# A graph kernel's edge stages: TensorE's counting and score loops written out, register lists loaded one group ahead, target parts in one matmul, slot writes spread from the bucket stage on

## The reference

```python
x = layernorm(x + L0(x))       # relu(W [x_src, x_tgt] + b), summed into the edge's source node
x = layernorm(x + L1(x))       # attention of 8 heads over the edges of a node, then layernorm
x = layernorm(x + L2(x))       # mean of the neighbours, two dense weights, layernorm
x = layernorm(x + L3(x))       # twice: gated relation weights, 2 relations mixed from 30 bases

def L1(x):                     # the scores that the change touches
    h = (x @ W.T).reshape(n, 8, 64)
    e_src = einsum('ehd,hd->eh', h[src], a_src)
    e_dst = einsum('ehd,hd->eh', h[dst], a_dst)
    e = leaky_relu(e_src + e_dst, 0.2) * (1 + et_emb[edge_type]) * edge_weight[:, None]
    # softmax of e over the edges of a node, weighted sum of h[src]

def rgcn(x, row, col, edge_type, basis, att, gate_w, root, bias):
    w = einsum('rb,bio->rio', att, basis)          # the mixing of the bases
    msg = where(edge_type == 0, gate_0 * x[col] @ w[0], gate_1 * x[col] @ w[1])
    return segment_sum(msg, row) + x @ root + bias
```

## Time and profile before

| | us |
|---|---|
| median of three runs | 1941.36 (1940.92 to 1942.94) |
| span of the profiled execution | 1934.6 |
| TensorE busy in it | 1608.4 (83%) |
| VectorE busy | 1167.7 (60%) |
| GpSimd busy | 705.2 (36%) |
| ScalarE busy | 471.2 (24%) |

### The profile page before, as it was taken

How to read it: one execution, slowest core, us unless ns; L and a number is a source line. 1 busy time by engine, 2 the same in 40 slices (tenths; PEclk the granted TensorE clock), 3 DMA queues, 4 the chain that set the end, 5 groups by cost and what they waited for, 6 DMA issues and landing times. The chain is left out here.

```text
span 1934.6 us, 27686 instructions
## 1 busy us (share of the span) xinstructions
PE 1608.4 (83%) x7565; PEld 981.3 (51%) x7566; DVE 1167.7 (60%) x2310; ACT 471.2 (24%) x884; POOL 705.2 (36%) x605
## 2 busy tenths in 40 slices
PE   6755956776498999998888459998498899999998
PEld 6751633335443555554555435554246545874486
DVE  5779958884365777775467766665774832113222
ACT  4301103432212555554344210000110111001100
POOL 0001877887094776660000347775330010000000
PEclk9997988998698999999899569999799999999999
DMA  0017844005802766682388337776104201430033
GB/s 25 0 47 285 275 136 120 1 1 172 306 27 92 210 197 187 187 169 45 126 317 331 101 100 211 210 209 171 27 1 144 96 1 72 155 122 1 0 136 135
DMA packets 76346, 248.96 MB, mean 129 GB/s; under 512 B 14901, under 2 KB 28582, under 8 KB 68346
## 3 DMA queue, kind: packets, MB, share of 16 engines
q1 hardware_dynamic: 38618, 147.08, 21.1%
q0 software_dynamic: 34592, 96.87, 18.9%
q10 hardware_dynamic: 3072, 4.20, 0.7%
HBM read 215.93 MB, written 32.00 MB: 128 GB/s over the span
## 5 line engine op out<-in xcount | busy, mean ns | idle before, releaser
L664 POOL DMA_INDIRECT tab_slots<-slot_words,slot_address x160 | 238.1, 1488 | 244.5 <-issue 233.3
L693 POOL DMA_INDIRECT e_rows<-tab_h,idx_h x176 | 178.6, 1015 | 293.4 <-POOLq L50 219.8
L1443 PE MATMUL dense_pY<-weights,dense_xT_block 128*128 128x512 f32 x640 | 284.3, 602 | 0.0
L1491 PE MATMUL dense_pY<-parts,dense_number 128*128 128x512 f32 x1000 | 237.7, 399 | 7.1 <-DMA dense_number<-tab_edges_to 7.1
L994 POOL DMA_INDIRECT e_rows<-tab_q,idx_q x192 | 182.0, 948 | 99.4 <-issue 38.9
L1491 PEld LDWEIGHTS dense_pY<-parts,dense_number 128*128 128x128 f32 x1000 | 188.7, 189 | 54.8 <-DMA dense_number<-tab_edges_to 8.6
L787 PE MATMUL e_pS<-e_rows,e_onehot_ring 128*128 128x512 f32 x352 | 194.2, 643 | 22.1 <-DVE e_rows L763 19.2
L1443 PEld LDWEIGHTS dense_pY<-weights,dense_xT_block 128*128 128x128 f32 x640 | 121.9, 194 | 143.1 <-issue 143.1
L1067 PE MATMUL e_pS<-e_rows,e_onehot_f 128*128 128x512 f32 x384 | 181.4, 596 | 0.0
L877 PE MATMUL count_pA<-count_onehot_d,count_onehot_s 128*128 128x512 f16 (+1 forms) x576 | 117.4, 352 | 63.8 <-DVE count_onehot_d L855 60.3
L763 DVE TENSOR_TENSOR e_rows<-e_rows,e_pW 128x1024 f32<-128x1024 f32 x88 | 107.3, 1220 | 69.3 <-DMA e_rows<-tab_h,idx_h 69.0
(11 more groups left out here) (312 smaller groups left out, 2448.4 us busy)
## 6 DMA issues: line engine op xcount, KB each, us to landing
basis_piece<-in_L_gnn_basis_pieces SPq DMA_DIRECT2D x32, 2048.0 KB, 7.9
dense_number<-tab_edges_from SPq DMA_DIRECT2D x20, 1280.0 KB, 5.4
tab_edges_from<-counts_turned SPq DMA_DIRECT2D x10, 1280.0 KB
tab_edges_to<-counts_total SPq DMA_DIRECT2D x10, 640.0 KB
dense_number<-tab_edges_to SPq DMA_DIRECT2D x10, 640.0 KB, 4.6
tab_w<-basis_wout ACTq DMA_DIRECT2D x128, 32.0 KB
weights<-tab_w SPq DMA_DIRECT2D x4, 1024.0 KB, 6.3
weights<-in_L_gnn_W_T SPq DMA_DIRECT2D x3, 1024.0 KB
```

The lines of the kernel that those rows point to most:

```text
L664: pool.indirect_dma_start(self.table, bass.IndirectOffsetOnAxis(self.address[:, t:t + 1], 0), self.words[:, t, :], None).then_inc(self.pla ...
L693: pool.indirect_dma_start(self.rows[:, q, s, :], None, self.table, bass.IndirectOffsetOnAxis(self.idx[:, j * 2 + s:j * 2 + s + 1], 0)).the ...
L1443: ins = self.nc.tensor.matmul(self.banks.at(g), self.xt[:, b % 2, c, :], weights[:, c, :], start=c == 0, stop=c == 3)
L1491: ins = self.nc.tensor.matmul(self.banks.at(self.first + b), self.number[:, b % 2, r * NB + k, :], self.parts[r][n][:, k, :], start=k == 0 ...
```

## The change

The diff has four edits. Slot writes: 24 of the 160 are issued by GpSimd in the bucket stage, 48 in placing, 68 in counting, 20 in storing. Counting: the ring of target one-hots grows from 4 to 8, TensorE's loop is written out over all 24 groups of eight tiles, and the registers of the next group are loaded behind the first tile of the current one. Scores: TensorE's loop is written out, and the target blocks of a step (eight registers) are loaded one step ahead in one go. Also there: the three parts of a target block stand side by side in memory, one matmul looks up all three, and VectorE adds them up while it takes them out.

```diff
-PLACED_WHILE_PLACING, PLACED_WHILE_COUNTING = 56, 144
+PLACED_WITH_BUCKETS, PLACED_WHILE_PLACING, PLACED_WHILE_COUNTING = 24, 72, 140
...
 def bucket_edges(
...
+        @block.gpsimd
+        def _(pool):
+            table.place(pool, 0, PLACED_WITH_BUCKETS)
...
 def count_edges(
-    RING, G, U = 4, 8, 16
+    RING, G, U = 8, 8, 16
...
-            def step(i):
-                for h in range(U // G):
-                    group = bass.ds(i * U + h * G, G)
-                    _, turn = nc.values_load_multi_w_load_instructions(
...
-            peeled(pe, SRC_SLOTS // U, step)
+            following = registers(0)
+            for g in range(SRC_SLOTS // G):
+                turn, bank = following
+                for u in range(G):
+                    t = g * G + u
+                    if u == 1 and t + G < SRC_SLOTS:
+                        following = registers(g + 1)
+                    pe.wait_ge(emptied, turn[u] & 31)
+                    pe.wait_ge(built, t + 1)
+                    for a, b in CH:
+                        ins = nc.tensor.matmul(flat(pA[:, bass.ds(bank[u], 1), a:b]), ohs[:, g % (U // G), u, :],
+                                               ohd[:, t % RING, a:b], start=False, stop=True, skip_group_check=True)
+                    ins.then_inc(done, 1)
...
 def edge_scores(
-        s3, d3 = sb("source3", [P, 3, NB, H], BF16), sb("target3", [P, 3, NB, H], BF16)
+        s3, d3 = sb("source3", [P, 3, NB, H], BF16), sb("target3", [P, NB, 3, H], BF16)
...
-                nc.vector.tensor_copy(ed_out[:, bass.ds(g * GS, GS), :],
-                                      pl[:, u % 2, ES:ES + ED].rearrange("p (s h) -> p s h", h=H))
+                nc.vector.tensor_reduce(ed_out[:, bass.ds(g * GS, GS), :],
+                                        pl[:, u % 2, ES:ES + ED].rearrange("p (s n h) -> p s h n", n=3, h=H),
+                                        AX.X, ALU.add)
...
-                blocks = [pe.value_load(pair_block[0:1, bass.ds(g * (GS // 2) + q, 1)], min_val=0,
-                                        max_val=NB - 1) for q in range(GS // 2)]
...
-                    for n in range(3):
-                        ins = nc.tensor.matmul(pl[:, u % 2, ES + s * H:ES + (s + 1) * H], ohT[:, u % 2, 1, s, :],
-                                               flat(d3[:, n, bass.ds(blocks[s // 2], 1), :]),
-                                               start=n == 0, stop=n == 2)
+                    block = blocks[u * (GS // 2) + s // 2]
+                    ins = nc.tensor.matmul(pl[:, u % 2, ES + s * 3 * H:ES + (s + 1) * 3 * H], ohT[:, u % 2, 1, s, :],
+                                           d3[:, bass.ds(block, 1), :, :].rearrange("p b n h -> p (b n h)"),
+                                           start=True, stop=True)
...
+            for i in range(STEPS):
+                before, blocks = blocks, following
+                for u in range(U):
+                    turn(i, u)
+                    if u == 2 and i + 1 < STEPS:
+                        following = blocks_of(i + 1)
```

More of the change, by code:

```diff
@@ L459, in _, with bucket_edges @@
                 peeled(pe, T // GT // 2, step)
-def bucket_edges(nc, name, C, key, rel, packed, pair_block, tile_bucket, tile_bank, bucket_end, pos_p, pos_s, value, basis):
+def bucket_edges(nc, name, C, key, rel, packed, pair_block, tile_bucket, tile_bank, bucket_end, pos_p, pos_s, value, basis,
+                 table):
     with ExitStack() as ctx:
@@ L597, in _ @@
         def _(pool):
-            table.place(pool, 0, PLACED_WHILE_PLACING)
+            table.place(pool, PLACED_WITH_BUCKETS, PLACED_WHILE_PLACING)
         @block.sync
@@ L881, in _, with registers @@
-            peeled(pe, SRC_SLOTS // U, step)
+            def registers(g):
+                group = slice(g * G, (g + 1) * G)
+                _, turn = nc.values_load_multi_w_load_instructions(
+                    tile_bucket[0:1, group], (mybir.EngineType.PE,), min_val=1, max_val=BUCKETS,
+                    skip_runtime_bounds_check_because="a sum of as many comparisons")
+                _, bank = nc.values_load_multi_w_load_instructions(
+                    tile_bank[0:1, group], (mybir.EngineType.PE,), min_val=0, max_val=1,
+                    skip_runtime_bounds_check_because="a single bit")
+                return turn, bank
@@ L1761, in edge_scores @@
     STEPS = SLOTS // GS // U
+    PAIRS_OF_STEP = U * GS // 2
     with ExitStack() as ctx:
@@ L1798, in _ @@
             split3(link, nc, [s3[:, n, :, :] for n in range(3)], est[:, :, :], rest[:, :, :])
-            split3(link, nc, [d3[:, n, :, :] for n in range(3)], edt[:, :, :], rest[:, :, :])
+            split3(link, nc, [d3[:, :, n, :] for n in range(3)], edt[:, :, :], rest[:, :, :])
             v.sem_inc(tables, 1)
@@ L1874, in turn, with blocks_of, look @@
                 ins.then_inc(turned, 1)
-            def look(i, u):
+            def blocks_of(i):
+                _, blocks = nc.values_load_multi_w_load_instructions(
+                    pair_block[0:1, i * PAIRS_OF_STEP:(i + 1) * PAIRS_OF_STEP], (mybir.EngineType.PE,), min_val=0,
+                    max_val=NB - 1, skip_runtime_bounds_check_because="a sum of as many comparisons")
+                return blocks
+            def look(i, u, blocks):
                 g = i * U + u
-                blocks = [pe.value_load(pair_block[0:1, bass.ds(g * (GS // 2) + q, 1)], min_val=0,
-                                        max_val=NB - 1) for q in range(GS // 2)]
                 pe.wait_ge(copied, g + 1)
```

17 lines of the change are left out of this document (8 added, 9 removed).

## The result

The changed kernel took 1919.37 us (median of four runs, 1914.21 to 1921.72) beside 1941.14 of the kernel before in the same runs: a ratio of 0.9894, 95% interval 0.9877 to 0.9911. Its profiled execution, timed at 1921.72, has a span of 1919.7 us.

The account below looks back on a forecast made before the run. Read stage by stage, whatever ends a stage last sets its time. Bucket +7.8, placing -11.9, counting -9.5, scores -8 make -21.6; 1934.6 - 21.6 + 6.8 gives 1920 us, own range 1914 to 1926, widened to 1908 to 1932.

Parts of the forecast that it names:

- The walk: Bucket stage: 24 slot writes traced one by one past VectorE's instructions, the last ending at 189.8 us; stage +7.8 us.
- writes run free: Rival, bucket stage: slot writes never wait for VectorE, so the +7.8 us is 0; 1912 us, chance 0.15.
- the reductions block too: Rival, bucket stage: VectorE's long one-input reductions also hold up slot writes, +17 instead of +7.8; 1929 us, chance 0.12.
- The bound of 0.5 us: Storing: four more writes put 500 small packets into busy DMA, costing up to 0.5 us; taken as 0.
- the group: Counting: eight TensorE tiles plus gap, 6.44 us on average, fall to 6.05, 24 times; -9.5 us.
- VectorE's floor of 5.67 us: Counting: VectorE's own least time per group of eight tiles, 5.67 us, below 6.05 and so not binding.
- VectorE waiting for TensorE nearly as before: Counting, sign expected in the changed profile: VectorE's waits for TensorE, 16.5 us before, hardly change.
- They need 121 us: Counting: the 68 slot writes left there take 121 us, ending some 20 us ahead of the stage.
- the forecast's -3: Scores, mixing steps: four groups take 12.1 instead of 12.5 us, held by landing loads and DMA; -3 us.
- the fourth rival: Scores: TensorE idles while DMA lands and its clock falls, +23 instead of -5; 1947 us, chance 0.05.
- a sign that the prediction gave for being wrong: Written-out stretches of TensorE's loops: the forecast is wrong if the granted clock drops there.
- The step of 6.8 us from span to median: Whole kernel: the median of 1941.36 lies 6.8 us above the profiled span of 1934.6; added to the forecast.

Follow-up runs that it names:

- store_none: Changed kernel with 24, 60, 76 and 0 slot writes, so none in storing; storing took 69.2 us, placing 111.1, counting 154.6.
- ring4: Changed kernel with counting's ring of target one-hots back at 4 instead of 8; counting took 163.5 us.
- tensor_only: Changed kernel with the old slot writes (none in bucket, 56 placing, 88 counting, 16 storing); 0.9955 of the kernel before, counting 165.1 us.
- one_load: Changed kernel with one of counting's two register loads gone, the bank worked out in TensorE's registers; 0.9901 of the kernel before, counting 157.0 us.
- warm: Changed kernel with 20 throwaway matmuls before TensorE's wait for each piece in the scores; 0.9885 of the kernel before, scores 127.5 us.
- best: Changed kernel with one_list, warm from the second mixing step, and 20, 48, 72, 20 slot writes; 1906.29 us, 0.9846 of the kernel before.
- one_list: Changed kernel with one load of 16 registers per counting group in place of two of 8; 0.9867 of the kernel before, counting 150.5 us.

## Why the prediction was right, and which of its terms were off

**Slot writes, bucket and placing: as forecast.** The walk held for the first fifteen writes: 3.43 us across L514, 6.48 across the scan, 1.18 beside L549. The sixteenth slipped in ahead of L564, so the seventeenth met it; those beside L567 took 1.18 again, and the last write ended 51.3 us into the stage (51.95 forecast). +7.2 and -12.1 stand beside +7.8 and -11.9. The rivals "writes run free" and "the reductions block too" are both excluded by these rows.

**Storing: +2.7 in the first profile where 0 was taken.** The bound of 0.5 us, from packets in a DMA that is busy anyway, was too small, but less so than +2.7 says. At 0.30 to 0.35 us a write (store_none) four more are worth 1.2 to 1.4. Two profiles with 16 writes took 73.6 and 74.8 us, eleven with 20 from 73.9 to 76.4; their means lie 1.0 apart.

**Counting: -7.0 where -9.5 was taken.** The mechanism is the one forecast: the two loads stay in TensorE's queue, the long gap goes, VectorE keeps up. The mis-sized term is the group: 0.4 us was taken, from a mean of 6.44 that includes the slow first group, down to 6.05; measured are 6.41 and 6.12, 0.29 us, 24 times. The gap itself fell by 0.38 us, from 1.60 to 1.22 on average, but the eight tiles, taken as 4.8 us before and after, went from 4.80 to 4.90; no run shows why. VectorE's floor of 5.67 us was too low as well (5.94), and the sign "VectorE waiting for TensorE nearly as before" did not come: 2.9 us for 16.5. The forecast took the gain from the written-out loop and gave the ring and the 20 writes no price of their own. ring4 and tensor_only show that each of them is a condition: without either, counting is slower than before. "They need 121 us" was read from the old kernel's write of 1.49; in the changed one a write takes 1.59 (107.83/68), and only because 68 are left is GpSimd done in time.

**Scores: -8 forecast, -6.6 in the first profile, -6 to -17 over seven of the same code.** Start and tail are steady: -3.1 and -4.6 us where -2 and -3 were taken. Between them the forecast's -3 is +1 in one profile and -9.5 in another (its 12.5 us for four groups should have been 12.7, by its own 3.18 a group). The mechanism is in part the one forecast: TensorE now waits for pieces, 18.6 to 22.7 us in the seven profiles where it was 2.3 and 1.9. This is also where the fourth rival lives, in small, and a sign that the prediction gave for being wrong did show: the granted clock dropped. It fell in up to five of 32 multiplies, not in most groups, and the stretch took up to ten us more than in the run in which it never fell; the rival had put +23 on the kernel before. DMA was not at its end there: in 20 us of the mixing steps the changed kernel moved 302 GB/s at a share of 0.81, one_load 390 at 1.00. That the falls lengthen the steps, and not only go with them, rests on warm and best, one profile each; what makes one run fall more often than another is open.

**The sum.** -21.6 was forecast; the medians moved by 21.8 and 20.1. The size came out closer than its parts: for counting it was 2.5 us too good and for storing 1 to 2.7, for bucket and placing together 0.8 too cautious, and for the scores, at -10 on average (130.5 us over those seven profiles, 140.5 in two of the old code), 2 us too cautious. That these errors cancel is luck. The step of 6.8 us from span to median was no constant: the changed kernel's profiled run lay 2.0 us above its span, so the profiled run of before was some 5 us under its median (one of 1936.38 us is among the four runs behind the 1941.14).

## What to carry to other kernels

In a program of stages with barriers, ask which engine ends each stage, and price a moved instruction in both stages; an edit that speeds one engine pays only when the next one to end, here GpSimd with 88 writes, has been relieved as well, so test the parts of a change apart and together. Small work that is moved under a long one is free only up to the last instruction that it must not outlive: 20 writes fitted into the bucket stage (49.2 us), and the last four cost 5 us. A loop in which TensorE waits for loads may give several times for one and the same code; look at the lengths of equal instructions before explaining the difference.

## What the runs showed of the hardware

- A slot write that met a VectorE instruction with two inputs in SBUF ended 0.99 to 1.06 us after it (6.48 us beside the scan); beside a reduction of one input it took 1.18, as when free. The Trainium skill (SBUF — State Buffer, section Who interferes with whom) has the second, and the traces agree. The same section has two inputs contend with what GpSimd reads; a slot write takes its addresses and words from tiles (`slot_address`, `slot_words`), so the 6.48 us fits that rule. Its inference that descriptor writing is not stalled by two inputs does not carry over to these writes; whether their reads or their descriptors were held up, no run separates.
- Loading one register into TensorE's sequencer took 0.30 us (scores before), eight 0.59 (counting), sixteen 1.10 (one_list); a register step beside the matmuls of one_load cost about 0.1.
- Of six waits of 2.16 to 2.65 us for a piece in the changed kernel's mixing steps, five were followed by a multiply at 1.2 GHz within the next two; in one_load, with no such multiply, one wait was over 2 us (3.09). So such waits went before the falls here, but did not settle them.
